# Two stacked matmuls per half instead of three, with the lo parts of x and of the weight chunks on GpSimd: a grouped conditional residual kernel

## The reference, cut to what matters

```
x = x + einsum('bct,bcd->bdt', x, W0[cond])      # 64x64 per sample
x = x + einsum('bsi,boi->bso', x, W1[adapter])   # 1024x1024 per adapter
```

## Time and profile before

| what | value |
|---|---|
| median of 3 runs | 830.72 us (828.99 to 831.37) |
| the profiled execution's own time | 828.85 us |
| its span | 827.1 us |
| PE busy | 808.9 us, 98% |
| DVE busy | 448.7 us, 54% |
| ACT busy | 279.2 us, 34% |
| POOL busy | 23.4 us, 3% |
| mean DMA rate | 110 GB/s |
| granted TensorE clock, mean | 0.998 |

### The profile page before, as it was taken

How to read it: one execution, slowest core, us unless ns; L and a number is a source line. 1 busy time by engine, 2 the same in 40 slices (tenths; PEclk the granted TensorE clock), 3 DMA queues, 4 the chain that set the end, 5 groups by cost and what they waited for, 6 DMA issues and landing times.

```text
span 827.1 us, 17869 instructions
## 1 busy us (share of the span) xinstructions
PE 808.9 (98%) x3580; PEld 669.5 (81%) x3581; DVE 448.7 (54%) x472; ACT 279.2 (34%) x515; POOL 23.4 (3%) x60
## 2 busy tenths in 40 slices
PE   4999999999999999999999999999999999999998
PEld 4888888788888888888888888888888888888886
DVE  6666666566765434666663466665443343343342
ACT  3323424333333323424333233333332332332232
POOL 1100000010000000000000000000000000000000
PEclk9999999999999999999999999999999999999999
DMA  6344343444433324444333444433332233232232
GB/s 212 105 119 151 121 140 96 126 128 139 138 104 88 98 79 121 124 146 122 109 101 83 119 122 145 129 106 95 93 101 61 89 94 83 77 101 78 75 101 76
DMA packets 73952, 90.88 MB, mean 110 GB/s; under 512 B 13780, under 2 KB 64468, under 8 KB 73940
## 3 DMA queue, kind: packets, MB, share of 16 engines
q1 hardware_dynamic: 63616, 57.45, 23.2%
q10 hardware_dynamic: 10324, 33.30, 15.2%
HBM read 57.15 MB, written 33.55 MB: 110 GB/s over the span
## 4 chain that ended last, share of the span: by engine, by line
PE 82%; DVE 5%; issue 2%; ACT 2%; DVEq 2%; ACTq 1%; SPq 1%; DMA 1%; POOL 0%; POOLq 0%
PE z_ps L467 12%; PE first_ps L467 12%; PE z_ps L468 12%; PE first_ps L468 12%; PE z_ps L470 12%; PE first_ps L470 11%; PE y_ps L481 3%; PE y_ps L482 3%; PE y_ps L483 3%; DVE w_turned L779 2%; DVE x_turned L794 2%; DVEq L206 1%; ACT xt_hi L572 1%; ACT w_hi L568 1%; DMA w_nat<-in_L_cond_weight_dram 1%
## 5 line engine op out<-in xcount | busy, mean ns | idle before, releaser
L467 PE MATMUL z_ps<-w_hi,xt_hi 128*128 (+1 forms) x528 | 205.6, 389 | 0.5 <-DVE xt_lo L803 0.5
L468 PE MATMUL z_ps<-w_lo,xt_hi 128*128 (+1 forms) x528 | 205.4, 389 | 0.0
L467 PE MATMUL first_ps<-w_hi,xt_hi 128*128 x528 | 205.4, 389 | 0.0
L468 PE MATMUL first_ps<-w_lo,xt_hi 128*128 x528 | 205.4, 389 | 0.0
L470 PE MATMUL z_ps<-w_hi,xt_lo 128*128 (+1 forms) x512 | 199.2, 389 | 0.0
L470 PE MATMUL first_ps<-w_hi,xt_lo 128*128 x480 | 186.7, 389 | 0.0
L794 DVE STREAM_TRANSPOSE x_turned<-x_in 128x1024 f32<-128x1024 f32 x66 | 141.5, 2144 | 26.2 <-issue 23.3
L572 ACT ACTIVATE xt_hi<-x_turned 128x1024 fp32r<-128x1024 f32 x66 | 70.0, 1061 | 234.1 <-DVE x_turned L794 229.1
L803 DVE TENSOR_TENSOR xt_lo<-x_turned,xt_hi 128x1024 fp32r<-128x1024 f32 x61 | 74.8, 1225 | 78.4 <-ACT xt_hi L572 78.4
L467 PEld LDWEIGHTS z_ps<-w_hi,xt_hi 128*128 128x128 f32 x528 | 99.1, 188 | 21.7 <-issue 0.9
L467 PEld LDWEIGHTS first_ps<-w_hi,xt_hi 128*128 128x128 f32 x528 | 99.1, 188 | 20.7
(11 more groups left out here) (137 smaller groups left out, 418.0 us busy)
## 6 DMA issues: line engine op xcount, KB each, us to landing
x_in<-in_x_dram SPq DMA_DIRECT2D x536, 64.0 KB, 2.0
out_dram<-y ACTq DMA_DIRECT2D x126, 256.0 KB, 3.1
w_nat<-in_L_cond_weight_dram SPq DMA_DIRECT2D x128, 128.0 KB
w_nat<-in_L_cond_weight_dram SPq DMA_DIRECT2D x4, 512.0 KB, 5.5
w_turned<-in_L_cond_weight_dram SPq DMA_DIRECT2D x2, 512.0 KB, 5.9
y<-in_L_cond_weight_dram SPq DMA_DIRECT2D x2, 512.0 KB, 8.1
x_turned<-in_L_cond_weights_dram SPq DMA_DIRECT2D x2, 256.0 KB, 4.0
x_in<-in_x_dram SPq DMA_DIRECT2D x2, 256.0 KB, 6.3
```

The source lines that it names most:

```text
L467: nc.tensor.matmul(to, xt_hi[h][:, t, :], whi, start=(t == 0), stop=False)
L468: mm = nc.tensor.matmul(to, xt_hi[h][:, t, :], wlo, start=False, stop=last and not pair)
```

## The change

1. **y by stacks.** For each sample k of a slot and each half n, z's hi part (64 rows) and lo part (64 rows) now lie above one another in one 128-row operand, `z_parts[:, n, k]`; the condition's hi and lo matrices lie side by side in one 128x128 weight, `w0_parts[:, k]`, copied whole from `w0_all`. One matmul gives W0hi·(z_hi+z_lo) in 64 rows of the bank and W0lo·(z_hi+z_lo) in the other 64. ScalarE copies one of the 64-row parts to y in SBUF (`begin_y`), VectorE adds the other out of PSUM (`finish_y`). So a slot has four y matmuls where it had six, and four y banks instead of two; `first_ps` at the start loses one of its two sets.
2. **lo parts on GpSimd.** `xt_lo` and the chunks' `w_lo` are made by GpSimd (`keep_xt_lo`, `keep_chunk_lo`). VectorE keeps `z_lo`, in two 64-row pieces for each half that write across the partitions, and the y sums. The transposes of x run a slot further ahead.
3. **x of slot 0** is loaded behind four chunks instead of six, when the two sample numbers are known (`samples_made`) and not the whole table.
4. The last y goes through the same `sum_y`, `begin_y` and `finish_y` as all others; the store of the slot before is issued after `z_hi` of half 1 also in the last slot.

```diff
-        w0_parts = sb("w0_parts", [P, 2, P], F32R)
+        w0_parts = sb("w0_parts", [P, 2, 2 * C], F32R)
-        z_hi = sb("z_hi", [P, NH, HALF], F32R)
-        z_lo = sb("z_lo", [P, NH, HALF], F32R)
+        z_parts = sb("z_parts", [P, NH, 2, HALF], F32R)
...
@@ gpsimd
+            def slot(s, h):
                 first, last = look(pool, s, CHUNKS_BEFORE, CHUNKS)
+                with pool.If(last > first):
+                    one_more_chunk(first)
+                keep_xt_lo(s + 1, 1 - h)
+                with pool.If(last > first):
+                    keep_chunk_lo(first)
...
@@ sync
-            for c in range(6):
+            for c in range(4):
                 load_first(c)
-            sp.wait_ge(table_made, 1)
+            sp.wait_ge(samples_made, 1)
...
-            for c in range(6, CHUNKS_PER_GROUP):
+            for c in range(4, CHUNKS_PER_GROUP):
                 load_first(c)
@@ tensor, sum_y
-                    pe.wait_ge(z_lo_made, NH * s + n + 1)
-                    to = y_ps[n][0:rows]
-                    nc.tensor.matmul(to, w0_slot[:, 0], z_hi[:, n], start=True, stop=False)
-                    nc.tensor.matmul(to, w0_slot[:, 0], z_lo[:, n], start=False, stop=False)
-                    nc.tensor.matmul(to, w0_slot[:, 1], z_hi[:, n], start=False, stop=True).then_inc(y_summed, 1)
+                    for k in range(2):
+                        pe.wait_ge(w0_placed, 2 * s + k + 1)
+                        pe.wait_ge(z_lo_made, PER_Z * s + 2 * n + k + 1)
+                        mm = nc.tensor.matmul(y_ps[n][k if pair else 0][:], w0_parts[:, k], z_parts[:, n, k],
+                                              start=pair or k == 0, stop=pair or k == 1)
+                        mm.then_inc(y_summed, 1)
@@ scalar
+                for k in range(2):
+                    nc.scalar.activation(z_parts[rows_of(k), n, k], z_banks[h][n][rows_of(k)],
+                                         ACT.Copy).then_inc(z_hi_made, 1)
...
+                def across(k, n, count):
+                    act.wait_ge(y_summed, PER_Y * s + 2 * n + 2)
+                    nc.scalar.activation(y[h][rows_of(k), n * HALF:(n + 1) * HALF], y_ps[n][k][rows_of(1 - k)],
+                                         ACT.Copy).then_inc(y_begun, count)
...
-                act.wait_ge(y_summed, NH * before + 1)
+                act.wait_ge(y_summed, PER_Y * before + 2)
                 keep_z_hi(s, h, 0)
...
+                act.wait_ge(y_summed, PER_Y * before + 4)
+                place_w0(s)
+                begin_y(before, 1 - h, stored)
                 keep_z_hi(s, h, 1)
+                store_y(before, 1 - h)
@@ vector
+                    dve.wait_ge(chunk_lo_made, k + (CHUNKS_PER_GROUP - 1))
                     nc.vector.transpose(
...
+                for k in range(2):
+                    dve.wait_ge(z_hi_made, PER_Z * s + 2 * n + k + 1)
+                    nc.vector.tensor_tensor(z_parts[rows_of(1 - k), n, k], z_banks[h][n][rows_of(k)],
+                                            z_parts[rows_of(k), n, k].bitcast(F32), ALU.subtract).then_inc(z_lo_made, 1)
...
+                    own = y[h][rows_of(k), n * HALF:(n + 1) * HALF]
+                    nc.vector.tensor_tensor(own, y_ps[n][k][rows_of(k)], own, ALU.add).then_inc(y_made, count)
...
-                turn_x(j + h, 1 - h)
-                keep_xt_lo(s + 1, 1 - h)
-                turn_chunks(first, last)
+                with dve.If(last > first):
+                    with dve.Fori(first, last) as k:
+                        turn_chunk(k)
                 keep_z_lo(s, h, 0)
-                place_w0_b(s)
+                finish_y(before, 1 - h)
+                turn_x(j + 1, h, xt_made=s + 1)
                 keep_z_lo(s, h, 1)
```

More of the change, by code:

```diff
@@ L183, in conditional_residual_kernel @@
         w0_lo_made = sem("w0_lo_made")
-        w0_placed = [sem(f"w0_placed{k}") for k in range(2)]
+        w0_placed = sem("w0_placed")
         z_summed = sem("z_summed")
@@ L240, in store_last @@
             with eng.If(stores > k):
[L241 to L244, removed]
+                for n in range(NH):
+                    eng.wait_ge(y_made, PER_Y * (2 * pairs_past + 1) + 2 * n + 1 + k)
+                    eng.dma_start(to[:, n * HALF:(n + 1) * HALF], y[1][rows, n * HALF:(n + 1) * HALF]
+                                  ).then_inc(last_stored, 16)
             with eng.Else():
@@ new lines, in one_more_chunk, with keep_chunk_lo @@
+            def one_more_chunk(k):
+                with pool.If(k % 2 < 1):
+                    pool.wait_ge(chunk_loaded[0], PER_CHUNK * (k // 2) + PER_CHUNK)
+                    add_1_to_chunk(0, k % CHUNKS_PER_GROUP)
+                with pool.Else():
+                    pool.wait_ge(chunk_loaded[1], PER_CHUNK * (k // 2) + PER_CHUNK)
+                    add_1_to_chunk(1, k % CHUNKS_PER_GROUP)
+            def keep_chunk_lo(k):
+                pool.wait_ge(chunk_hi_made, k + 1)
+                nc.gpsimd.tensor_tensor(of_chunk(w_lo, k), turned(k), of_chunk(w_hi, k).bitcast(F32),
+                                        ALU.subtract).then_inc(chunk_lo_made, 1)
@@ L314, in add_1_to_chunks @@
+            def slot(s, h):
                 first, last = look(pool, s, CHUNKS_BEFORE, CHUNKS)
                 with pool.If(last > first):
[L316 to L323, removed]
+                    one_more_chunk(first)
+                keep_xt_lo(s + 1, 1 - h)
+                with pool.If(last > first):
+                    keep_chunk_lo(first)
+                with pool.If(last > first + 1):
+                    with pool.Fori(first + 1, last) as k:
+                        one_more_chunk(k)
+                        keep_chunk_lo(k)
@@ L530, in y_last @@
             def y_last(pair):
[L531 to L542, removed]
+                pe.wait_ge(y_made, PER_Y * (2 * pairs_past + 1))
+                sum_y(2 * pairs_past + 1, pair)
             for_both(stores, y_last)
@@ L800, in keep_xt_lo @@
                 stores, = look(dve, s, STORES)
                 with dve.If(stores > 1):
-                    dve.wait_ge(xt_hi_made, s + 1)
-                    nc.vector.tensor_tensor(xt_lo[h][:], x_turned[h][:], xt_hi[h][:].bitcast(F32),
-                                            ALU.subtract).then_inc(xt_lo_made, 1)
+                    for n in range(NH):
+                        for k in range(2):
+                            add(k, n, 2 * n + k + 1, 1)
                 with dve.Else():
-                    dve.wait_ge(xt_hi_made, s + 1)
@@ L817, in keep_z_lo, with slot @@
-            def keep_z_lo(s, h, n):
-                dve.wait_ge(z_hi_made, NH * s + n + 1)
-                nc.vector.tensor_tensor(z_lo[:, n], z_banks[h][n][:], z_hi[:, n].bitcast(F32), ALU.subtract).then_inc(z_lo_made, 1)
-            def slot(j, h):
+                    for n in range(NH):
+                        add(0, n, 2 * n + 2, 2)
+            def slot(j, h, before):
                 s = 2 * j + h
                 first, last = look(dve, s, CHUNKS_BEFORE, CHUNKS)
-                turn_x(j + h, 1 - h)
-                keep_xt_lo(s + 1, 1 - h)
-                turn_chunks(first, last)
+                with dve.If(last > first):
+                    with dve.Fori(first, last) as k:
+                        turn_chunk(k)
```

166 lines of the change are left out of this document (77 added, 89 removed).

## The result

| what | value |
|---|---|
| the changed kernel, median of 5 runs | 823.68 us (822.31 to 825.88) |
| the kernel before, median of 5 runs beside it | 831.34 us (828.99 to 831.84) |
| ratio | 0.9911, interval 0.9895 to 0.9927 |
| span of the profiled execution | 822.0 us (before 827.1) |

What follows compares the result with a forecast made beforehand. TensorE, busy 98% of the span, was taken as the bound. Span 827.1 - 29.4 - 1.2 - 0.5 + 3.5 + 5.5 = 805.0, 806.7 as that execution's time, stated as 807 us; forecast 804 to 815, range 800 to 821.

Steps and rivals of the forecast that it cites:

- Matmuls: On TensorE, two matmuls fewer per slot, 130 x 0.226 us over 65 slots: -29.4 us.
- GpSimd: One add and two subtractions per chunk slot, at most 7.9 us, under the slot's 11.75: cost 0, no block expected.
- the signs: What the changed profile should show, including GpSimd subtractions of 2 to 3.7 us and some 5 us of `z_lo` waits.
- Start: At the kernel's start, z begins near 26.9 instead of 28.10, -1.2 us; the wait on `xt_lo` goes, -0.5 us.
- End: After the last `z_hi`, copies and sums of y finish at +6.1 us; the end grows by 3.5 us.
- The ring closes at 12.2 us: In chunk slots, a circle of VectorE and ScalarE steps takes 12.2 us against TensorE's 11.75, losing 0.45 per slot.
- +5.5 us: Total stall from the chunk-slot circle: 4.0 us in the first group, 0.5 in each of the other three.
- The upper bound: The stall's upper case, 17 us: ScalarE too waits out its forerunner when rows change, 0.12 at some three places.
- The first group: First group of chunk slots: first delivery 0.9 us late, then 7 x 0.45, a loss of 4.0 us.
- The clock stays at the upper level: TensorE's clock stays at the upper level because TensorE runs without gaps; 0.226 us per matmul.
- the formula: Loss of each later group: eight times the circle's excess over a slot, less 3.1 us slack; 0.5 us forecast.
- The ring is longer: Rival: the chunk-slot circle takes 12.75 us, 23 us of stalls in all, time 822 to 826; chance 0.15.

Runs made afterwards that it cites:

- lo_only: The kernel before, with only the lo parts of x and chunks moved to GpSimd, y still by three matmuls per half; 830.71 us, ratio 0.9990.
- the control: The changed kernel with only a max with 0 in a register added to three table numbers; 825.0 us, ratio 0.9927 to the kernel before.
- ring_cut: The control with ScalarE's copy `w_hi` of a chunk moved behind the copies of y; 805.71 us, ratio 0.9686 to the kernel before.
- rows_grouped: The control with the four copies and four sums of y done sample by sample instead of half by half; 817.7 us, ratio 0.9831.

## Why the prediction was wrong

- *Matmuls*, -29.4: right. Its 0.226 us for a matmul is 100/443 of the earlier trace rows, at a granted clock of 1.00. 132 fewer; 443 in 100 us wherever nothing waits, the clock at 1.00 there too (600:700); no wait of PE on `z_lo` once the chunks are done.
- *GpSimd*, 0: right, 2.40 us inside the bounds 1.23 and 3.7. No block in the changed kernel: the longest of its 93 large subtractions took 2.42. The reason I gave for that, no second SBUF tensor among VectorE's inputs, is not shown: the copy that `lo_only` shows held up reads one SBUF tensor. The lower end of 2 us among the signs was an estimate, which no row shows; the runs showed 2.40.
- *Start*, -1.2 and -0.5: the wait on `xt_lo` went, and the other term came true in the control alone. z began at 26.91 there, as forecast, but at 29.19 in the profiled execution, 1.1 later than before. The forecast took one execution's arrivals for fixed. The share of the DMA engines was full in both, at different rates, in the window 16 to 20 us of the change and then of the kernel before (what made the rates differ stays open):

```profile
16.00:20.00 4.00, 1.97 (x8) 1.57 (x8) 1.93 (x3) 1.74 (x4) 0.83 (x2) 1.00 1.02 194
```
```profile
16.00:20.00 4.00, 2.93 (x16) 2.73 (x14) 3.42 (x6) 3.12 (x6) 0.46 (x1) 1.00 1.04 308
```

- *End*, +3.5: measured +4.1. The last y matmul came 1.7 later behind z, and copies and sums instead of one copy took 2.9 more; 0.5 came back in the stores. That the number is so near is in part luck: the last sum ended 7.2 behind the last `z_hi` and not 6.1. The forecast let ScalarE copy y as soon as its stores were issued (+2.65); they were issued by 814.35, but reading the table and branches held ScalarE until the last y was there too, +3.7:

```profile
814.85 0.75 ACTq L205
```
```profile
815.79 2.44 ACT L603 ACTIVATE y<-y_ps 64x512 f32<-64x512 f32 x4 [2.48 <-PE y_ps L505]
```

- **The step that failed: "The ring closes at 12.2 us", and with it the "+5.5 us".** The ring was there, at the place named, and `ring_cut` shows that it is nearly all of the loss (18.9 of the control's 20.9 us). Its length is 12.54. VectorE's terms were right (sums 2.88 for 2.84, transpose 2.16 for 2.17, z_lo 1.44 for 1.42); a 64x512 sum or `z_lo` took 0.69 (mean), as 128x512 did in the earlier trace rows. ScalarE's were not: `w_hi` to `z_hi` 1.09 for 0.97, two pieces of `z_hi` up to the next instruction 1.23 for 0.94; `w_parts` gave back 0.22. I had read ScalarE's 0.47 between instructions that all begin at partition 0, and used it for pieces that alternate between lower and upper rows, although I had counted 0.71 for each such piece on VectorE, from the L815 row. That explains the 1.23, which holds two changes of rows, 0.13 each by `rows_grouped`. It does not explain the 1.09: `w_hi` and the first piece both begin at row 0, and no run isolates that 0.12. The upper bound had it ("ScalarE too waits out its forerunner when rows change"); the likeliest value did not. The bound's 0.12 for a change was an estimate that no row of the trace before shows on ScalarE; `rows_grouped` showed 0.13. There and in the change a 64x512 copy is 0.59 us long (mean of 256): the four take 2.43 with three changes of rows, more than 4 x 0.59 = 2.36, so each waits for its forerunner's end, and 2.16 with one, so there they overlap. 0.3 us in 32 slots is 10 us, because a ring already above the slot passes all of it on. Stalls were 14.4 us over the forecast, the start 2.3 and the end 0.6: together 17.3, where 17.0 lie between the forecast 806.7 and that execution's 823.68.
- The first group was counted wrongly besides. It lost 9.9 us against 4.0. First, its last chunk slot meets a slot of a single sample, where TensorE asks again after 24 + 16 + 4 = 44 matmuls, 9.97 us, and not 11.79:

```profile
145.00 0.61 PE L505 MATMUL y_ps<-z_parts,w_parts 128*128 128x512 f32 x2
147.11 0.50 PE L505 MATMUL y_ps<-z_parts,w_parts 128*128 128x512 f32 x1 [1.49 <-DVE z_parts L822]
```

  That one wait is 2.57 us. Second, the first delivery was 2.20 late and not 0.9, and the granted clock fell behind it. PE's two pieces of y, then two windows behind them:

```profile
57.40 0.61 PE L505 MATMUL y_ps<-z_parts,w_parts 128*128 128x512 f32 x2
59.27 0.51 PE L505 MATMUL y_ps<-z_parts,w_parts 128*128 128x512 f32 x1 [1.25 <-DVE z_parts L822]
```
```profile
62.00:64.00 2.00, 2.00 (x6) 1.61 (x5) 0.12 (x1) 1.32 (x2) 1.17 (x1) 0.50 0.16 54
...
66.00:68.00 2.00, 2.00 (x11) 1.64 (x10) 1.94 (x3) 1.87 (x4) 0.70 (x1) 1.00 0.64 160
```

  At 62 the granted clock is 0.50 and the next 24 matmuls took 7.19 us instead of 5.44: 1.75 more. "The clock stays at the upper level", which was 1.00 in the earlier trace rows, was wrong here. But these 1.75 us are not part of the loss in the end. The chunk's transpose came back at the same distance through the slow stretch:

```profile
47.39 2.19 DVE w_turned L799
...
59.97 2.17 DVE w_turned L799
...
72.50 2.17 DVE w_turned L799
...
85.02 2.17 DVE w_turned L799
```

  TensorE's slow stretch filled time in which it would have waited for this circle: the next slots, from 73.14 to 96.71, have no stall at all. In the control the first delivery was 1.54 late, the clock stayed at 1.00 between 54 and 62 us, and the first group lost 9.7 us, as much as here. Nor did the 2.57 us at 145 us bring the clock down: it read 1.00 from 144 to 156 us.
- For the later groups the formula held: 8 x (12.54 - 11.79) - 3.1 = 2.9, measured 3.3. The rival *The ring is longer* (chance 0.15) described what happened. That its 822 to 826 us hold the measured 823.68 is in part luck: it needed a ring of 12.75, and the measured 12.54 got there with the first group's extras. Of the signs named, PE's waits on `z_lo` were 8.5 us and not 5, and in all four groups. The range's upper end assumed 12.6 and no such extras.

## What to carry to other kernels

When work is spread over engines in a circle, compare the circle's length with the time of the bound engine for one turn; if the two are within a few per cent, its terms must be right to a tenth of a microsecond, and pitches must be read between instructions of the same rows and operands (a change of rows cost 0.12 us on VectorE and 0.13 on ScalarE here). A busy share of 99% hid a late circle here (428 matmuls where 443 fit): count matmuls in equal windows, and look for a line of another engine that returns at a fixed distance in the chain that ended last. The cure is to ask which step of the circle nobody in it needs; here that was `w_hi`, worth two thirds of the matmuls removed.

## What the runs showed of the hardware that was not expected

- ScalarE, like VectorE, overlaps two 64-row instructions less when the start partition changes: four copies of y last 2.43 us with three changes and 2.16 with one, 0.13 for each change. VectorE's four sums last 2.85 and 2.61, 0.12 for each.
- GpSimd's 2.40 us subtraction holds up VectorE's copy of 64x128 between two SBUF tensors, 1.83 us instead of 0.22.
- One late operand can bring the clock down, but need not: after 2.20 us of waiting at one y the granted clock was 0.50 and the next 24 matmuls took 1.75 us more; after 1.54 us in the control, and after 2.57 us later in the same execution, it stayed at 1.00, so the length of the wait alone does not tell. In this kernel the lower clock cost nothing in the end, since the circle set the pace.
